# Preparing quantized feed-forward weights: scale products on VectorE, transposes by DMA, modulation products first

## The reference

```
scale = max(max(abs(xb)) / 6, 1e-12)              # per block of 16 of the last dim
q = GRID[searchsorted(MID, abs(xb / scale))] * sign(xb) * scale
gate = einsum(q(x), q(w_gate)); y = einsum(q(x), q(w_up))
h = silu(gate) * y
out = einsum(q(h), q(w_down))
...
h = layernorm(x) * (1 + cb) + sb
x = x + gb * ffn(h, w_gate, w_up, w_down)         # |gb| held at 0.25 or more
```

## Time and profile before

| what | value |
|---|---|
| median of 3 runs | 4145.38 us (4139.29 to 4150.52) |
| the profiled execution | 4149.2 us, its span 4147.4 us |
| busy in the span: TensorE, VectorE, ScalarE, GpSimd | 87%, 81%, 42%, 22% |
| attention, up to | about 2525 us |
| weight preparation | about 2525 to 2682 us |
| feed-forward loop | from 2682 us |

### The profile page before, as it was taken

One profiled execution on the slowest core, in us unless ns is written; L12 is line 12 of the kernel. 1 busy time (PEld: TensorE's weight loads), 2 busy tenths in 40 slices (PEclk: granted clock), 3 DMA queues, 4 the chain that ended last, 5 costly groups with the idle time before them and its releaser, 6 DMA issues. The chain is left out here.

```text
span 4147.4 us, 151943 instructions
## 1 busy us (share of the span) xinstructions
PE 3600.3 (87%) x64072; PEld 2405.7 (58%) x64072; DVE 3358.0 (81%) x7542; ACT 1735.4 (42%) x3493; POOL 918.9 (22%) x737
## 2 busy tenths in 40 slices
PE   4889899898888888888988984299999999999998
PEld 3777677676676676776776762144444444444443
DVE  4788788887888877788887867878888888888887
ACT  2434444344344343443443412344444444444443
POOL 1122222221222222122221213522222222222221
PEclk7999999999999999999999986599999999999999
DMA  4000010000000000000000012023323323323322
GB/s 118 13 24 29 19 34 18 24 28 19 24 28 20 32 19 24 29 19 24 28 24 29 13 69 75 5 69 77 87 74 82 84 72 86 81 75 86 79 77 73
DMA packets 325485, 195.99 MB, mean 47 GB/s; under 512 B 265152, under 2 KB 265920, under 8 KB 324800
## 3 DMA queue, kind: packets, MB, share of 16 engines
q1 hardware_dynamic: 324800, 186.07, 16.2%
HBM read 89.56 MB, written 33.55 MB: 30 GB/s over the span
## 5 line engine op out<-in xcount | busy, mean ns | idle before, releaser
L932 DVE COPY_PREDICATED Am<-pick,banks 128x64 f32<-128x64 uint8 (+2 forms) x1792 | 461.2, 257 | 127.6 <-DVE Am L932 12.4
L764 POOL TENSOR_TENSOR raw_up<-raw_up,raw_gate 128x1024 f32<-128x1024 f32 x128 | 312.4, 2440 | 1084.9 <-DVE raw_up L814 1084.9
L1623 PE MATMUL fbank<-gT,xqT 128*128 128x464 f16 (+1 forms) x2304 | 491.4, 363 | 68.9 <-DVE h L1502 45.9
L1623 PE MATMUL fbank<-uT,xqT 128*128 128x464 f16 (+1 forms) x2304 | 487.7, 361 | 1.8 <-issue 1.7
L1632 PE MATMUL fbank<-dT,hqT 128*128 128x512 f16 x2112 | 467.8, 380 | 8.0 <-DMA hqT<-hq 8.0
L530 PE MATMUL banks<-raw_up,raw_gate 128*128 128x256 f32 x2048 | 459.0, 383 | 1.8 <-DVE xxx L827 1.8
L530 PEld LDWEIGHTS banks<-raw_up,raw_gate 128*128 128x128 f32 x2048 | 386.7, 191 | 54.2 <-issue 2.1
L1623 PEld LDWEIGHTS fbank<-gT,xqT 128*128 128x128 f16 x2304 | 221.2, 98 | 320.0 <-DVE h L1502 70.7
L1623 PEld LDWEIGHTS fbank<-uT,xqT 128*128 128x128 f16 x2304 | 225.4, 98 | 233.5 <-issue 3.1
L775 POOL TENSOR_TENSOR yrs<-yvar,neg_half 128x32 f32<-128x32 f32 x32 | 174.0, 5437 | 834.3 <-DVE yvar L961 834.3
L1632 PEld LDWEIGHTS fbank<-dT,hqT 128*128 128x128 f16 x2112 | 207.1, 98 | 255.9 <-DMA hqT<-hq 8.5
(11 more groups left out here) (234 smaller groups left out, 7204.5 us busy)
## 6 DMA issues: line engine op xcount, KB each, us to landing
raw_scale<-in_L_attn_x SPq DMA_DIRECT2D x32, 512.0 KB, 3.7
xres<-in_L_attn_x SPq DMA_DIRECT2D x32, 512.0 KB, 3.7
x_after_attention<-xres SPq DMA_DIRECT2D x32, 512.0 KB, 3.4
xl<-x_after_attention SPq DMA_DIRECT2D x64, 256.0 KB, 2.7
xr<-x_after_attention SPq DMA_DIRECT2D x64, 256.0 KB, 2.7
out<-xr SPq DMA_DIRECT2D x64, 256.0 KB, 2.1
raw_gate<-in_L_ffn_w_gate SPq DMA_DIRECT2D x1, 2816.0 KB, 11.3
raw_up<-in_L_ffn_w_up SPq DMA_DIRECT2D x1, 2816.0 KB, 18.5
```

Of the source, the lines that this page charges most:

```text
L764: nc.gpsimd.tensor_tensor(xf[:, j % NXF].rearrange("p g b t -> p (g b) t"), xf[:, j % NXF].rearrange("p g b t -> p (g b) t"), hT[:, :, :, ...
L932: nc.vector.copy_predicated(dst, mask, src).then_inc((done or A_step).sem, 1)
L1623: last = nc.tensor.matmul(GU[2 * pair + t][:, 0:w], xqT[:, u, a, g, :], W[:, b_, g, lo_:hi_], start=(k == 0), stop=(k == 3 * G - 1))
```

## The change

The products with the scale parts leave GpSimd. ScalarE writes both parts of the block scales out in full as 16-bit values (`full_scales`), and VectorE multiplies two dense 16-bit tiles (`part_of`), item n-1 between the steps of item n. So that a part of the scale is exact in 16 bits, the constant that splits it becomes `SPLIT`. High and low land side by side in `parts`, and one transposing DMA from SyncE's queue per item puts them into the weights. TensorE's transposes and ScalarE's copies out of PSUM are gone, and with them the identity. TensorE makes all modulation products at the start; two of their three inputs are loaded into the still unused `dT`.

```diff
-            s_low, s_high = ts("s_low", [P, 3, nbw]), ts("s_high", [P, 3, nbw])
+            s_low, s_high = ts("s_low", [P, 2, nbw]), ts("s_high", [P, 2, nbw])
-            q16, hi, lo = ts("q16", [P, 2, I_FF], F16), ts("hi", [P, 2, I_FF], F16), ts("lo", [P, 2, I_FF], F16)
+            q16, parts, full = ts("q16", [P, 2, I_FF], F16), ts("parts", [P, 2, 2 * I_FF], F16), ts("full", [P, 2, 2, I_FF], F16)
-            mods = [mod_w[:], raws[0][:, 0:G], raws[0][:, G:2 * G]]
+            early_mods = dT[:].rearrange("p a k n -> p (a k n)")[:, 0:4 * G * C].bitcast(F32).rearrange("p (m g n) -> p m g n", m=2, g=G)
+            mods = [early_mods[:, 0], early_mods[:, 1], raws[0][:, 0:G]]
...
-                    sp.dma_start(ident, ident_in).then_inc(small_loaded.sem, 16)
                     load_mod(0)
+                    load_mod(1)
                     sp.dma_start(raws[2][:], w_down.rearrange("(r p) k -> p r k", p=P)).then_inc(early.loaded[2].sem, 16)
-                    for m in range(1, 3):
-                        sp.wait_ge(a_done.sem, m * G)
-                        load_mod(m)
+                    for n, (t, r) in enumerate(items):
+                        if t == 2 and r == 0:
+                            sp.wait_ge(modf_done.sem, 6)
+                        sp.wait_ge(parts_done.sem, 2 * (n + 1))
+                        dst = (gT, uT, dT)[t][:, :, :, r * P:(r + 1) * P].rearrange("p a k n -> p (a k) n")
+                        sp.dma_start_transpose(dst, parts[:, n % 2, 0:2 * width(n)]).then_inc(wT_landed[n % 2].sem, 16)
+                        if n == G - 2:
+                            sp.wait_ge(a_done.sem, G)
+                            load_mod(2)
+                    for p in range(2):
+                        sp.wait_ge(wT_landed[p].sem, 8 * len(items))
...
+                    def full_scales(n):
+                        t, r = items[n]
+                        w, (view, spread) = width(n), blocks_of(n)
+                        act.wait_ge(scale_step.sem, scale_step.at(t))
+                        if n >= 2:
+                            act.wait_ge(parts_done.sem, 2 * (n - 1))
+                        for part, scale in enumerate((s_high, s_low)):
+                            nc.scalar.activation(view(full[:, n % 2, part, 0:w]), spread(scale, t % 2), ACT.Copy).then_inc(full_done.sem, 1)
...
-                        if not first(n):
-                            evacuate(n - 1)
-                        if n + 1 == len(items) or first(n + 1):
-                            evacuate(n)
+                        full_scales(n)
...
-                    for n, (t, r) in enumerate(items):
-                        if r == 0:
-                            pool.wait_ge(wmax_done.sem, t + 1)
-                            nc.gpsimd.partition_all_reduce(wall[:, t:t + 1], wmax[:, t:t + 1], P, bass.bass_isa.ReduceOp.max).then_inc(all_max.sem, 1)
...
+                    for t in range(3):
+                        pool.wait_ge(wmax_done.sem, t + 1)
+                        nc.gpsimd.partition_all_reduce(wall[:, t:t + 1], wmax[:, t:t + 1], P, bass.bass_isa.ReduceOp.max).then_inc(all_max.sem, 1)
...
+                    def part_of(n, part):
+                        w, p = width(n), n % 2
+                        dve.wait_ge(q_done.sem, n + 1)
+                        dve.wait_ge(full_done.sem, 2 * n + part + 1)
+                        if n >= 2:
+                            dve.wait_ge(wT_landed[p].sem, 16 * (n // 2))
+                        V.tensor_tensor(parts[:, p, part * w:(part + 1) * w], q16[:, p, 0:w], full[:, p, part, 0:w], ALU.mult).then_inc(parts_done.sem, 1)
...
                         V.scalar_tensor_tensor(a, m, GRID, a, ALU.max, ALU.add).then_inc(s_done.sem, 1)
+                        if n > 0:
+                            part_of(n - 1, 0)
                         dve.wait_ge(s_done.sem, n + 1)
-                        if n >= 2:
-                            dve.wait_ge(lo_done.sem, n - 1)
                         V.scalar_tensor_tensor(q16[:, p, 0:w], m, GRID, a, ALU.max, ALU.subtract).then_inc(q_done.sem, 1)
...
+                        if n > 0:
+                            part_of(n - 1, 1)
+                    for part in range(2):
+                        part_of(len(items) - 1, part)
```

More of the change, by code:

```diff
@@ L1081, with feed_forward @@
 HEAD = 256.0
-def feed_forward(nc, out, x1, w_down, c_in, wmod, ident_in, early, nt=2 * NI):
+SPLIT = 2.0 ** 14 + 1.0
+def feed_forward(nc, out, x1, w_down, c_in, wmod, early, nt=2 * NI):
     with ExitStack() as ctx:
@@ L1158, in blocks_of @@
                 view = lambda ap: ap.rearrange("p (n k) -> p n k", k=NB)
-                spread = lambda scale: scale[:, t, r * nb:(r + 1) * nb].unsqueeze(2).to_broadcast([P, nb, NB])
+                spread = lambda scale, at=t: scale[:, at, r * nb:(r + 1) * nb].unsqueeze(2).to_broadcast([P, nb, NB])
                 return view, spread
@@ L1305, in _ @@
+                    for part in range(2):
+                        part_of(len(items) - 1, part)
                 @blk.tensor
                 def _(pe):
[L1307 to L1316, removed]
-                            if k == G - 1:
-                                last.then_inc(modf_done.sem, 1)
@@ L1320, in _ @@
-                    for n, (t, r) in enumerate(items):
-                        p = n % 2
-                        pe.wait_ge(hi_done.sem, n + 1)
-                        pe.wait_ge(lo_done.sem, n + 1)
-                        if n >= 2:
-                            pe.wait_ge(wT_used.sem, n - 1)
-                        if t == 2 and r == 0:
-                            pe.wait_ge(row_done.sem, 2)
-                            pe.wait_ge(gate_step.sem, 9)
-                        for part, src in enumerate((hi, lo)):
-                            for k in range(G if t < 2 else KF):
-                                if t < 2:
-                                    ps, x = bank[6 + p], part * G + k
-                                elif k < 8:
-                                    ps, x = bank[3 * p + part], k
-                                else:
-                                    ps, x = bank[3 * p + 2], part * 3 + k - 8
-                                last = nc.tensor.transpose(ps[:, x * P // 2:(x + 1) * P // 2].bitcast(F16), src[:, p, k * P:(k + 1) * P], ident16[:])
-                        last.then_inc(wT_done.sem, 1)
-                        for m, first in enumerate(MOD_FIRST):
-                            if first <= n < first + 4:
-                                mod_part(m, n - first)
@@ L1343, in feed_forward @@
+                    pe.wait_ge(c_ready.sem, 1)
+                    pe.wait_ge(cb_ready.sem, 1)
+                    for m in range(3):
+                        pe.wait_ge(mod_loaded[m].sem, 16)
+                        for b in range(B):
+                            for k in range(G):
+                                last = nc.tensor.matmul(mod_bank[m][b][:], c_b[:, b, k, :], mods[m][:, k, :], start=(k == 0), stop=(k == G - 1))
+                            last.then_inc(modf_done.sem, 1)
         GU = bank[0:4]
@@ L1712, in adaln_rwkv6_fp4_ffn @@
                   c_in, wmod, ident_in, diag_in, pick_in, w_gate, w_up, early)
-        feed_forward(nc, out, x1, w_down, c_in, wmod, ident_in, early)
+        feed_forward(nc, out, x1, w_down, c_in, wmod, early)
 _INS = ["L0_attn_x", "L0_attn_time_maa_x", "L0_attn_time_maa_wkvrg", "L0_attn_tm_w1", "L0_attn_tm_w2", "L0_attn_time_decay",
```

42 lines of the change are left out of this document (5 added, 37 removed).

## The result

The changed kernel takes 4121.25 us (median of 5 runs, 4107.86 to 4124.51) against 4150.52 us (5 runs, 4139.29 to 4156.39): a ratio of 0.9928, interval 0.9905 to 0.9951. The medians differ by 29.3 us; by the interval the gain lies between 20 and 39 us.

What follows compares the result with a forecast made beforehand. GpSimd was taken to set the pace, by its products and by slowing VectorE. Stage terms summed to 111.8 us against 146.7, 34.9 less; minus 2.3 for GpSimd's return, 32.6 off 4145.4 gave 4113 us, range 4105 to 4124.

Steps and rivals of the forecast that it cites:

- Items: VectorE's row blocks of gate, up and down matrices: 26.95, 27.65 and 25.9 us, before 37.8, 36.4 and 34.1.
- Scales: Scales of the up matrix: 5.9 us instead of 12.3, the 5.6 us wait for the second all-reduce gone.
- Middle: Gate row, block maximum and scales of the down matrix: unchanged, 18.1 us.
- Transposing DMAs: Landings behind VectorE's products: mostly hidden, 1.8 us lost in sum, bounds 0 and 10.
- The room: Time from an item's second product until its buffer is wanted again: 3.55 us, 2.35 where items lack the scaling product.
- Tail: From VectorE's last product to SyncE's first load of the next stage: 5.5 us instead of 8.0.
- GpSimd's return: Configuration instruction before the next stage's first rstdf: a 7.1 us gap starts it 2.3 us later.
- Longer landings: Rival, 15%: 8-block transposes land after about 4.5 us, 8 us of the gain go back; about 4121 us.
- The 11.2 us switch: Rival, 8%: GpSimd's return to ordinary products costs an 11.2 us gap, 4.1 us more; 4117 us.
- The stride: Rival, 3%: strided destination breaks the transposes down, kernel slower than before; 4175 us at sixfold landing cost.
- The sum for blocks that go one by one: Transposes at 1309 ns a block: 264 blocks take 346 us instead of 112, kernel some 4380 us; the trace disagrees.
- That contention was not GpSimd's: Rival, 2%: VectorE's steps stay near 1.5 us, the stage about as long as before; 4145 us.

Runs made afterwards that it cites:

- e3: Changed kernel plus 22 GpSimd products on constants, which nobody waits for, beside the items of the up matrix; 4146.46 us.
- e2: Changed kernel with GpSimd's products put back, leaving only transposing DMAs and early modulation products new; 4152.99 us against 4142.65 for the kernel before.
- e5: Changed kernel with the third modulation load behind the last transpose of the gate matrix instead of behind the third; 4124.13 us.
- e8: Changed kernel with e5, e6 and e7 together; median 4112.54 us, ratio 0.9934 to the kernel before.
- e9: e8 with the third modulation load one transpose earlier, behind that of item 9; median 4115.19 us, ratio 0.992 to the kernel before.
- e7: Changed kernel with two transposes of 11 blocks for each down item, the high part sent as soon as made; 4115.55 us.
- e6: Changed kernel plus one tiny ordinary GpSimd product behind the last all-reduce, so the configuration instruction stands inside the stage; 4110.73 us.
- e4: Changed kernel with transposing DMAs writing blocks side by side into contiguous destinations, so the output is not the reference's; 4126.67 us.

## Why the prediction was right

The forecast was 4113 us with a range of 4105 to 4124; 4121 lies in it. Of the 8.4 us between them, 5.1 come from the starting point, a median of 4145.38 us over three runs that became 4150.52 over five; only 3.3 are a smaller gain (29.3 instead of 32.6). Step by step:

- **Items.** Forecast without waits 26.95, 27.65 and 25.9 us. Measured, with the waits taken off, 29.66 - 2.6 = 27.1, 28.51 - 0.9 = 27.6 and 26.40 - 0.6 = 25.8. The step was right because both prices came from rows: undisturbed starts 0.60 us apart, and the 16-bit products of the loop at 425 and 892 ns. e3 shows the cause of the old pace, e2 that nothing else in the change removes it. ScalarE, which I had as a possible new limit, never became what VectorE waits for in after.
- **Scales.** 5.9 forecast, 5.88 measured. The wait of the earlier trace rows is gone. **Middle.** Unchanged, 18.1.
- **Transposing DMAs: the term that was mis-sized most.** Waits for landings are 4.1 us instead of 1.8. One wait makes half of the excess: 2.06 us at item 5, behind the modulation load, for which I had 0.9. I had let 1024 KB hold the queue for 3.1 us and the transpose land after 4.4; the load itself took 5.8 to land (its row among after's issues, below) and a transpose behind it 5.6, which less the 3.55 us of room is the wait. The room was right, the landing was not. One place in the down matrix, for which I took nothing, gave 0.6, the two short items gave 1.0 where I had 0.9, and the slow first transpose of the up matrix 0.4 more. e5 and e8 move the wait with the load, and e9 takes it away: 3.7 us of waits in e8, 1.4 in e9. (The 0.6 of the down matrix had gone with e7's split.) Whether a transpose is late because it stands behind the load in SyncE's queue or because the load's traffic runs beside it, no run separates: none puts the load on another queue.

```profile
raw_gate<-in_L_wmod SPq DMA_DIRECT2D x1, 1024.0 KB, 5.8
...
dT<-parts SPq DMA_TRANSPOSE x4, 5.2
```

- **Tail.** 6.8 us instead of 5.5. I had priced the landing of 22 blocks at 4.7; it took 5.2 (and 5.1 to 5.4 over the four). I had let the neighbour cost 0.8, at most 1.3: the issue before it, 3.3 us long, holds the last one back from 2628.63 to 2629.7, so 1.1 us. The rest, some 0.4 us from the landing to SyncE's first load, was not in my sum at all. e7 halves the transposes and gets 5.83.
- **GpSimd's return.** The configuration instruction did move in front of `rstdf`, at 3.0 us instead of 2.3 (7.82 - 4.85). e6 takes back 2.9 of them with one spare instruction, so this is shown and not argued. The gap itself was 6.84 us, in that kernel. The Trainium skill (GPSIMD Engine Reference, Instruction dispatch) speaks of some 6 us of code loading at the first call to a freshly loaded kernel; the gaps here are 6.0 us in front of an all-reduce and 6.8 to 7.2 on the way back (7.5 in e3, where GpSimd's first span is rough), so the same or 1 to 1.5 us more. The 11.2 us behind the first all-reduce come again in e2 (10.99) and stay unexplained: that the load of the down matrix beside it is the reason was argued and not tested.
- **Sum.** 28.4 instead of 32.6 us: 2.3 of landings, 1.3 of tail, 0.7 of the return, less 0.1 of rounding. The medians' difference of 29.3 agrees, but its interval (20 to 39 us) would hold 32.6 as well; what was mis-sized is shown by the profiles.
- **The rivals.** Longer landings: its 4121 us is what was measured, but by chance. It wanted 8.2 us more of waits, spread over some 20 items; 2.3 more came, in five waits in all, none of them from the stride, and the largest behind one load. The 11.2 us switch: not here. The stride: refuted by e4. The sum for blocks that go one by one, 4380 us, was wrong in itself: 346 instead of 112 us are 234 more than the changed kernel's 4113, some 4350, and not more than before's 4145. With 8 blocks landing in 3.0 us the 1309 ns that the Trainium skill (VectorE: DVE Perf Modes, The three transpose paths) gives for one 128x128 block is no price for a transpose of many; a single block was not run here. That contention was not GpSimd's: refuted by e3.
- **Luck.** That the loop keeps its pace I had assumed. Its first twelve matmuls take 4.19 us after (4.06 before), and from the first `rstdf` to the fifth it takes 72.8 us after and 72.9 before, so it starts at the same pace. Over the twelve profiles the whole loop lies between 1460.1 and 1464.0 us. The four shortest (before, e6, e8, e9) are kernels in which nothing holds the first `rstdf`, but the fifth of that kind, e2, took 1463.5, and after itself 1462.8 and then 1461.2; whether 1 or 2 us of that belong to the change can't be told.

## What to carry to other kernels

When VectorE's instruction shows two durations for one shape, look at what GpSimd does beside the longer one before counting instructions: adding two dense 16-bit products to VectorE and idling GpSimd made an item shorter by 1.0 us here. A transposing DMA was priced here by three numbers, its issue on the queue's engine, its landing, and what large load had gone out just ahead of it; where a load is to go is decided by when the parts of the transposes around it come, not by item numbers. And where a change is worth less than the executions scatter, cut the span at fixed instructions: the stage repeated within 0.02 us while executions of the same kernel lay 15 us apart.

## What the runs showed of the hardware

- The issue of a transposing DMA grows with its blocks and not in proportion: 8 blocks 1.23 us, 11 blocks 1.39, 22 blocks 3.33; with contiguous destinations (e4) 8 blocks take 1.23 and 22 blocks 3.39. They land 3.0, 3.5 and 5.2 us after their issue (medians).
- GpSimd's products slow VectorE's two-input instructions, and the 16-bit ones too: 0.68 to 1.54 us in 32 bits, 0.42 to 1.27 in 16 bits (e3). One instruction with a single tensor input was slow beside them as well: 1.19 us where after has 0.34.
- GpSimd pays its "issue" gap also on the way back from all-reduces to ordinary products (6.84 us), at the next product, however much later that comes.
- The start of the stage, behind attention that is the same code, lies between 2520.1 and 2527.8 us in two executions of one kernel, and between 2520 and 2546 over all twelve profiles.
